# Two attention layers over a graph on one core: turning the weights with VectorE blocks and quadrant DMAs instead of TensorE, in a program without loops

## The reference

```python
def _gat_layer(x, W, adj):
    proj = x @ W
    Wh, Ws = jnp.split(proj, 2, axis=-1)
    scores = Wh @ Ws.T
    a = jax.nn.softmax(scores, axis=-1) * adj
    out = a @ Wh
    out = out + x
    return jax.nn.leaky_relu(out, NEG_SLOPE)
...
for l in range(W_stack.shape[0]):
    x = _gat_layer(x, W_stack[l], adj)
...
x = _layernorm(x + _L0_gnn_ref(x, adj, L0_gnn_W_stack), axis=-1)
```

## Time and profile before

| | |
|---|---|
| time, median of 3 runs | 1793.34 us (1793.21 to 1793.46) |
| span of the profiled execution | 1791.6 us, 31961 instructions |
| time of the profiled execution around its span | not given apart; the median of the runs is 1.7 us above the span |
| TensorE (matmul) busy | 1770.0 us, 99% |
| VectorE busy | 1293.3 us, 72% |
| ScalarE busy | 787.6 us, 44% |
| GpSimd busy | 120.7 us, 7% |
| granted TensorE clock, mean | 0.998 of full speed |
| moved by DMA | 196.40 MB, 110 GB/s |

### The profile page before, as it was taken

How to read it: one execution, slowest core, us unless ns; L and a number is a source line. 1 busy time by engine, 2 the same in 40 slices (tenths; PEclk the granted TensorE clock), 3 DMA queues, 4 the chain that set the end, 5 groups by cost and what they waited for, 6 DMA issues and landing times.

```text
span 1791.6 us, 31961 instructions
## 1 busy us (share of the span) xinstructions
PE 1770.0 (99%) x10152; PEld 1519.4 (85%) x10152; DVE 1293.3 (72%) x2406; ACT 787.6 (44%) x1767; POOL 120.7 (7%) x199
## 2 busy tenths in 40 slices
PE   8999999999999999999999999999999999999997
PEld 8988888888888888888898888888888888888886
DVE  5677777776777776767666777777777777777776
ACT  5544444444444444444365444444444444444442
POOL 0000000000000000000000001100110010011001
PEclk9999999999999999999999999999999999999999
DMA  6533333233333333333264333333333333333331
GB/s 205 166 105 104 101 100 104 94 103 100 103 99 102 102 105 100 100 105 100 68 230 145 94 118 109 96 103 112 110 99 108 111 111 99 108 111 104 95 113 39
DMA packets 70614, 196.40 MB, mean 110 GB/s; under 512 B 8640, under 2 KB 16832, under 8 KB 70592
## 3 DMA queue, kind: packets, MB, share of 16 engines
q1 hardware_dynamic: 62912, 175.14, 31.3%
q0 software_dynamic: 7680, 20.98, 3.4%
HBM read 171.97 MB, written 24.12 MB: 109 GB/s over the span
## 4 chain that ended last, share of the span: by engine, by line
PE 98%; DVE 1%; DMA 0%; ACT 0%; issue 0%; POOL 0%; SPq 0%; ACTq 0%; DVEq 0%; POOLq 0%
PE banks L429 27%; PE banks L286 15%; PE banks L287 15%; PE banks L288 15%; PE banks L432 13%; PE banks L412 12%; PE banks L321 1%; DMA load<-x_scratch 0%; DVE q_t L553 0%; DMA ring<-w 0%; DVE moving_lo L553 0%; PE banks L296 0%; ACT moving_hi L533 0%; ACT q_t L494 0%; DVE rows L664 0%
## 5 line engine op out<-in xcount | busy, mean ns | idle before, releaser
L429 PE MATMUL banks<-wh,moving_hi 128*128 128x512 f32 x2048 | 787.9, 419 | 0.1
L516 ACT ACTIVATE ring<-banks,neg_max 128x512 f32<-128x512 f32 x512 | 353.0, 690 | 766.3 <-DVE neg_max L607 766.1
L553 DVE TENSOR_TENSOR moving_lo<-banks,moving_hi 128x512 fp32r<-128x512 f32 x545 | 376.9, 691 | 396.3 <-ACT moving_hi L533 393.5
L432 PE MATMUL banks<-wh,moving_lo 128*128 128x256 f32 x2048 | 575.4, 281 | 0.0
L429 PEld LDWEIGHTS banks<-wh,moving_hi 128*128 128x128 f32 x2048 | 385.8, 188 | 70.0 <-DVE moving_lo L553 0.8
L286 PE MATMUL banks<-x_t,q_t 128*128 128x512 f32 x1024 | 404.1, 395 | 0.4 <-DVE q_t L553 0.4
L287 PE MATMUL banks<-x_t,q_t 128*128 128x512 f32 x1024 | 401.4, 392 | 0.0
L288 PE MATMUL banks<-x_t,q_t 128*128 128x512 f32 x1024 | 399.9, 391 | 0.0
L642 DVE SCALAR_TENSOR_TENSOR ring<-ring,weight,load 128x512 f32<-128x512 f32 x512 | 381.3, 745 | 16.6 <-issue 9.0
L432 PEld LDWEIGHTS banks<-wh,moving_lo 128*128 128x128 f32 x2048 | 389.3, 190 | 0.0
L533 ACT ACTIVATE moving_hi<-banks 128x512 fp32r<-128x512 f32 x512 | 306.2, 598 | 176.1 <-PE banks L432 176.1
(11 more groups left out here) (66 smaller groups left out, 791.1 us busy)
## 6 DMA issues: line engine op xcount, KB each, us to landing
load<-adj SPq DMA_DIRECT2D x256, 512.0 KB, 4.0
qt_scratch<-q_t SPq DMA_DIRECT2D x30, 512.0 KB, 3.0
q_t<-qt_scratch SPq DMA_DIRECT2D x60, 256.0 KB, 4.2
load<-x SPq DMA_DIRECT2D x16, 256.0 KB, 3.2
rows<-x POOLq DMA_DIRECT2D x32, 128.0 KB, 4.0
x_scratch<-rows POOLq DMA_DIRECT2D x32, 128.0 KB, 2.0
load<-x_scratch SPq DMA_DIRECT2D x16, 256.0 KB, 3.0
rows<-x_scratch POOLq DMA_DIRECT2D x32, 128.0 KB, 3.4
```

The source lines that it names most:

```text
L429: nc.tensor.matmul(psum[:, bank, :], moving_hi[:, slot % 2, of], wh[:, j].rearrange("p a d -> p (a d)"), start=start, stop=stop, skip_grou ...
L432: last = nc.tensor.matmul(psum[:, bank, 0:D], moving_lo[:, slot % 2, of], wh[:, j, 0], start=False, stop=stop, skip_group_check=True)
L516: nc.scalar.activation(ring[:, slot, :], psum[:, SCORE_BANK + k % SCORE_BANKS, :], ACT.Exp, bias=neg_max[:, slot:slot + 1], accum_out=chun ...
L553: return nc.vector.tensor_tensor(out_ap, value, as_f32(hi), ALU.subtract)
```

## The change

The kernel is written anew around the same arithmetic. What is different:

- **Chunks of 1024 columns** (two PSUM banks) instead of 512: the maximum, the exponential and the weighing take 1024 columns in one instruction, 128 steps for a layer instead of 256. A tile has 4 chunks.
- **The weighed chunk is no longer turned on TensorE.** VectorE transposes its 32 x 32 blocks in place (`turn_blocks`), and eight DMAs on the SP queue, each of 32 partitions x 512 columns (64 KB), carry the blocks to their place in `turned` (`move_blocks`). Two chunks make a unit of 2048 columns; a block of `turned` holds columns 64 apart from one 32-row piece to the next, and `wh` is made in the same order of columns (`pick_columns` on GpSimd).
- **The parts of the turned weights.** ScalarE copies 4 blocks (512 columns) of `turned` from SBUF into `a_hi`. The subtraction for `a_lo`, which was VectorE's, is GpSimd's (`split_a`), and each one first waits until VectorE has weighed the chunk of that step (`a_done`).
- **No loops.** Every engine's program is written out in full. `LAG_WEIGH` is 4 steps, `LAG_PRODUCT` 7, `LAG_ROWS` 11.
- **The projections move into the pipeline.** Only the transposes of x (8 groups of 512 rows) stand ahead of the scores. `wh` (2 tiles at a time) and `q_t` (2 tiles at a time, kept on chip, no scratch) are "sides" of 12 matmuls of 256 columns each: two `wh` sides in each of the first 8 steps of layer 0; in layer 1 eight of them together at step `LATE_GROUP` (the fourth step of the layer) and two in each of the four steps after it; a `q` side every 8 steps. The second layer's weights wait in an HBM scratch.
- **Between the layers** four steps have products but no scores; in them seven of the eight groups of layer 1's input are loaded and transposed, the eighth at `LATE_GROUP`.
- **All DMAs are on the SP queue**, the rows' loads and stores too. GpSimd has no DMA left.

```diff
-    CHUNK = 512
+    BANK = 512
+    CHUNK = 2 * BANK
...
-                def transpose_a(pair, k):
...
-                    for b in range(BLOCKS):
-                        last = nc.tensor.transpose(psum[:, AT_BANK + slot % 2, b * P:(b + 1) * P],
-                                                   ring[:, slot, b * P:(b + 1) * P], ident[:])
...
+            def turn_blocks(i):
+                dve.wait_ge(a_done, i + 1)
+                nc.vector.transpose(ring[:, i % RING, :], ring[:, i % RING, :]).then_inc(blocks_turned, 1)
...
+            def move_blocks(i):
+                unit, c = i // 2, i % 2
+                u = unit % 2
+                sp.wait_ge(blocks_turned, i + 1)
+                if unit >= 2:
+                    sp.wait_ge(lo_done, SUB * (unit - 1))
+                for q in range(2 * c, 2 * c + 2):
+                    for r in range(QUADS):
+                        sp.dma_start(as_f32(turned[QUAD * q:QUAD * (q + 1), u, r]).rearrange("p b j -> p (b j)"),
+                                     ring[QUAD * r:QUAD * (r + 1), i % RING, (q - 2 * c) * BANK:(q - 2 * c + 1) * BANK]
+                                     ).then_inc(moved[u][q], 16)
...
+                i = chunk_at(step - LAG_WEIGH)
+                if i is not None:
+                    move_blocks(i)
+                    if i + 2 < LAYERS * CHUNKS:
+
+                        load_adj(i + 2)
...
-                    low(moving_lo[:, slot % 2, :], psum[:, AT_BANK + slot % 2, :],
-                        moving_hi[:, slot % 2, :]).then_inc(at_lo, 1)
...
+            def split_a(step, j):
+                unit, b = j // SUB, j % SUB * SUB
+
+                weighed = chunk_at(step - LAG_WEIGH)
+                if weighed is not None:
+                    pool.wait_ge(a_done, weighed + 1)
+                pool.wait_ge(hi_done, j + 1)
+                nc.gpsimd.tensor_tensor(
+                    a_lo[:, j % 2].rearrange("p b (r j) -> p b r j", r=QUADS),
+                    as_f32(turned[:, unit % 2, :, b:b + SUB, :]).rearrange("p r b j -> p b r j"),
+                    as_f32(a_hi[:, j % 2]).rearrange("p b (r j) -> p b r j", r=QUADS),
+                    ALU.subtract).then_inc(lo_done, 1)
```

More of the change, by code:

```diff
@@ new lines, in tile_at, with x_groups_at, sides_before @@
+        def tile_at(step):
+            for layer in range(LAYERS):
+                n = step - layer * OFFSET
+                if n >= 0 and n % CPT == 0 and n // CPT < TILES:
+                    return layer * TILES + n // CPT
+            return None
+        def x_groups_at(step):
+            n = step - CHUNKS
+            if 0 <= n < 4:
+                return [GROUPS + g for g in range(2 * n, min(2 * n + 2, GROUPS - 1))]
+            return []
+        def sides_before(step):
+            return [("wh", WPAIRS + v) for v in range(WPAIRS // 2)] if step == LATE_GROUP else []
@@ L281, in _ @@
+            for p in range(2):
+                sp.wait_ge(rows_stored[p], 16 * TILES)
         @block.tensor
```

942 lines of the change are left out of this document (490 added, 452 removed).

## The result

The changed kernel took **1933.63 us** (1932.53 to 1934.27) against 1793.34 before: ratio 1.078, 95% interval 1.076 to 1.080. The forecast was 1717 with a range to 1830. It is 7.8% slower where 4.3% faster was forecast, and it lies outside the range, on the side of rival 1. (A ratio is the time over that of the kernel before; the figures behind it are its 95% interval.)

What follows compares the result with a forecast made beforehand. TensorE, busy 99%, was taken as the bound; start 28 + steps 1428 + sides 92 + edges 114 + between layers 27 + end 26 = 1715 us of span, 1717 us with 1.7 around it; range 1655 to 1830.

Steps and rivals of the forecast that it cites:

- rival 1: SP's loop replaces TensorE as bound, slower once its round trip passes 12.5 us; chance 0.19, plus 0.10 between 12.1 and 12.5.
- The issue of a move: SP's queue: 0.42 us per issue, eight issues 3.4 us of the 11.6 us round trip for two steps.
- `adj` behind them: The adj load issued behind the eight moves on SP: 512 KB landing in 4.2 us, plus 0.1 wake.
- The slope: Each us of SP round trip over 11.6 adds 1.8 us per tile in layer 0, 1.0 in layer 1: 87 us.
- Rival 3: Each 64 KB move holds SP's queue 0.95 us instead of 0.42: round trip 15.8 us, time 2082 us; chance 0.03.
- TensorE's step, 5.58: TensorE's own work in a step, two chunks of scores and two products: 5.58 us, 256 steps 1428 us.
- The transposes' 220 us: TensorE's transposes of the weighed chunks (L412), which the change takes away: 0.43 us per chunk, 220 us.
- The edges, 1.25 and 2.43 us: TensorE's stall per tile edge through GpSimd's wait, layers 0 and 1, each with 0.3 for SP's loop: 114 us in all.
- Start 28 us: Before the first scores, only x transposes and two weight preparations stand ahead: 28 us (25 to 32).
- End 26: After the last scores, the last tile's weighing, moves, product, finishing and store beyond TensorE's remaining work: 26 us.
- Between the layers: Extra time there for x groups' load, transposition and splits, and GpSimd's column picking: 27 us (18 to 40).
- Costed at nothing: Loop branches, `q_t`'s trips to HBM and the 134 MB of block moves as such: no time added.

Runs made afterwards that it cites:

- run 5: The changed kernel with each of its eight moves per chunk cut to half its bytes (32 KB), same number of DMAs: 1903.94 us.
- run 6: The changed kernel with four moves of 128 KB per chunk in place of eight, the same bytes in half the DMAs: 1753.91 us.
- run 4: The changed kernel with adj loaded from ScalarE's queue, SP keeping the moves and the rows: 1757.69 us.
- run 13: On run 4's kernel, GpSimd's wait for the weighing dropped only between the layers and at layer 1's tile edges: 1732.54 us.
- run 7: On run 4's kernel, GpSimd's wait dropped only in steps that weigh a tile's first chunk (the edges): 1759.69 us.
- run 8: On run 4's kernel, GpSimd's wait for the weighing dropped in every step: 1763.38 us.
- run 2: The changed kernel with GpSimd's wait for the weighing dropped, nothing else edited: 1898.81 us.

## Why the prediction was wrong, point by point

- **The issue of a move: the step that failed.** "An issue: 0.42 us from one to the next (61.90 to 62.32), 0.58 for four in a row (2.31 / 4) ... I take 0.42: 3.4." Eight moves took 4.95 us, 0.62 each. The earlier trace rows held the answer: the moves are DMAs in a row, and the row for DMAs in a row said 0.58. I took the gap behind a single issue, although only the row of four had the changed kernel's pattern, and leaned on the guess that fewer bytes would take less issue; runs 5 and 6 show that bytes don't enter.
- **`adj` behind them.** Taken 4.3 with its wake. The round shown has 5.0 from the start of the issue to the weighing, but it is a late one: over the 97 loads of this place that the weighing waited for, the median is 4.5. The landing of the earlier trace rows is counted from the start of the issue (the load of 608.36 landed 4.92 us later), so the load's own issue is in it. With 4.95 - 3.4 = 1.6 and 0.7 here the round trip is 13.9 instead of 11.6, and 13.95 was seen; of the median round's excess, 13.6 - 11.6, the issues are three quarters.
- **The slope was near, in part by luck.** 87 us for each us of round trip gives 1717 + 87 x 2.35 = 1921; measured 1933.6. Against run 4's kernel, which is free of the loop, the loop costs 1933.6 - 1757.7 = 176 us, 75 for each us of that round; a tile 3.31 us in layer 0, where 1.8 x 2.35 = 4.2 were forecast, and 2.55 in layer 1, where 1.0 x 2.35 = 2.4 were. The forecast's start from 1717 was some 40 us too low, and that made up for the slope. Rival 1's rule and its place held, and so did its first sign, the weighing that waits for `adj`. Its turning point, 12.5 us, was not measured; with 1757.7 and 75 it would lie near 12.1. Its chance was too small: the sum stood within 0.9 us of the point where the sign turns, and the upper bound of one row alone, 0.58, passed it. Rival 3 took the time of one transfer for the time that its issue holds the queue: a move lands 2.0 us after its issue starts (median), and the next is issued after 0.63.
- **TensorE's step, 5.58:** 5.59 where nothing waits (run 4). **The transposes' 220 us:** gone from TensorE, but most of it comes back as waits: run 4's kernel, free of the loop, is 36 us faster than the kernel before, run 13's 61.
- **The edges, 1.25 and 2.43 us:** in run 4's kernel 24.02 - 22.36 - 0.72 = 0.94 and 25.89 - 22.36 - 0.72 = 2.81. Without the 0.3 for SP's loop, which that kernel doesn't have, the forecast was 0.95 and 2.13: right in layer 0, 0.7 us too short in layer 1. As a cause it was half right. I put the edges down to the wait, and without it they stay (runs 7, 8).
- **Start 28 us:** first maximum 1.9 us late. **End 26:** 3 late.
- **Between the layers: 27 us were too few by 19.** I added the x groups' latency to the steps, but neither the new wait nor the clock. After:

```profile
936.28 2.36 DVE L541 TENSOR_TENSOR x_t<-banks,x_t 128x1024 fp32r<-128x1024 f32 x2 [7.74 <-ACT x_t L459]
938.55 1.28 DVE L605 SCALAR_TENSOR_TENSOR ring<-ring,weight,load 128x1024 f32<-128x1024 f32 x1
```
```profile
939.91 2.50 POOL L695 TENSOR_TENSOR a_lo<-turned,a_hi 128x512 fp32r<-128x512 f32 x2 [10.07 <-DVE ring L605]
```
```profile
928.66 0.80 PE L395 MATMUL banks<-wh,a_hi 128*128 128x512 f32 x1 [4.91 <-POOL a_lo L695]
...
933.95 2.11 PE L331 MATMUL banks<-ident,ring 128*128 128x128 f32 x16
941.23 0.80 PE L395 MATMUL banks<-wh,a_hi 128*128 128x512 f32 x1 [5.17 <-POOL a_lo L695]
...
945.65 1.91 PE L331 MATMUL banks<-ident,ring 128*128 128x128 f32 x16
```

  The weighing is queued behind the splits of x, GpSimd stands 10.07 us until it is done, the last 2.3 of them with its high part ready (ScalarE ends it at 937.6), TensorE 5.17, and the next transposes of x stand behind that product: a loop of some 12 us (933.95 to 945.65), where 6.5 were forecast. The wait is only part of it, those 2.3 us in each round: without it the time between the layers falls by 5 us (55.4 to 50.5 from after to run 2, 58.9 to 53.6 from run 4 to run 8). In run 13's kernel, which has no wait there, the loop still takes 9.5 us, from one group of transposes to the next:

```profile
831.52 1.91 PE L328 MATMUL banks<-ident,ring 128*128 128x128 f32 x16
...
841.03 1.91 PE L328 MATMUL banks<-ident,ring 128*128 128x128 f32 x16
```

  There GpSimd waits for ScalarE, whose high parts stand behind its copies of x. The clock is another part: after the idle time of 4.91 us the granted clock is 0.50 from 928 to 934 us, the lower of its two levels (1.2 of 2.4 GHz), and the product there takes 933.95 - 928.66 = 5.29 us, where the forecast had 2.83. The four products of this place take 19.4 us together instead of 11.3, so some 8 of the 19 us missing are an estimate of the clock's part.
- **Costed at nothing:** the 134 MB of moves as bytes: right (run 5: half of them less, 30 us, where half the count gave 180). TensorE's clock: not right. The granted clock was 1.00 before and 0.97 to 0.98 in the two layers' stages after, with the idle time between the products, and 0.80 from 910 to 960 us, between the layers; the same 8104 matmuls are busy for 1646.4 us after and for 1602.0 in run 4's kernel. It is in the tiles' times above.
- **What of the 0.59 us belongs to the row of DMAs ahead:** 0.08. The first move of a group of eight lasts 0.51 at the median and the seven behind it 0.59 each, in 244 groups. For a load of `adj` it is more: 0.33 with nothing just ahead and 0.58 behind other DMAs. That is the row ahead and not the queue, since on SP before, and on ScalarE's queue in run 4, the load alone took the same:

```profile
L257 SPq DMA_DIRECT2D load<-adj x256: 328/333/1639, 62.3 to 1757.1; - x128
```
```profile
L527 ACTq DMA_DIRECT2D load<-adj x254: 334/335/378, 56.6 to 1722.0; - x127
```

  Why a move alone takes 0.51 where the eight times larger load takes 0.33 stays open; the shape (32 partitions to 32 others) and the place it reads from differ, and no run parts them.

## What to carry to other kernels

When a change replaces one engine's work by many small DMAs, count issues and not bytes, price them by the row that has several in a row on the same queue, and follow what is issued behind them: here a load that the next steps needed stood behind eight moves which waited for the steps' last result, and moving that one line was worth 162 us. When a computed loop lies within its own error of another bound, the forecast's chance belongs on both sides of it. A wait that keeps two engines apart should be judged place by place: it paid in layer 0, where it spared VectorE some 2 us at an edge, and cost 5 us between the layers, where the waited-for work is queued behind something else.

## What the runs showed of the hardware

- A DMA's issue on SP has a median of 591 ns at 32, 64 and 128 KB from 32 partitions to 32 others (512 for the first of a group), some 0.62 us from one to the next; two queues issue side by side at that price (2.51 us for four on SP while ScalarE's four took 2.46).
- A 512 KB load with nothing just ahead of it took 335 ns to issue on ScalarE's queue and 333 on SP; behind moves on SP 582.
- VectorE's instruction of four elements a partition took 1.29 us instead of 0.23, and the weighing 2.27 instead of 1.28, while a GpSimd subtraction ran. Over the whole kernel without the wait the weighing's mean rose from 1284 to 1702 ns.
- GpSimd's subtraction of 128x512 with both inputs in SBUF takes 1283 ns, VectorE's block transpose of 128x1024 fp32 1245 ns.
